# Rounding of quantised weights moved to ScalarE, activation tables loaded at named points, six tiles of a norm on ScalarE

## The reference, cut to what matters

```
x = x + tanh(g_xattn[l]) * xattn_l(layernorm(x), ctx_1024, ...)
x = x + tanh(g_ffn[l])   * ffn_l(layernorm(x), ...)
```

```
wq = clip(round(w / s_w), -128, 127) * s_w      # s_w = max|w| of the row / 127
xq = clip(round(x / s_x), lo, hi) * s_x         # s_x from the maximum of all of x
h  = silu(xq @ Wgate) * (xq @ Wup)              # layer 1 (352 hidden features)
h  = relu(xq @ W1 + b1)                         # layer 2 (512 hidden features)
y  = quantised(h) @ quantised(Wdown or W2)
```

## Time and profile before

| | |
|---|---|
| three runs | 1810.07, 1813.54, 1822.59 us, median 1813.54 us |
| the profiled execution | 1814.86 us, its span 1813.0 us |
| busy in the span | PE 72%, PEld 51%, DVE 64%, ACT 48%, POOL 24% |
| mean granted TensorE clock | 0.863 of full speed |
| table loads on ScalarE | 19 of 1283 ns |

### The profile page before, as it was taken

One profiled execution on the slowest core, in us unless ns is written; L12 is line 12 of the kernel. 1 busy time (PEld: TensorE's weight loads), 2 busy tenths in 40 slices (PEclk: granted clock), 3 DMA queues, 4 the chain that ended last, 5 costly groups with the idle time before them and its releaser, 6 DMA issues. The chain is left out here.

```text
span 1813.0 us, 32142 instructions
## 1 busy us (share of the span) xinstructions
PE 1304.0 (72%) x12243; PEld 922.2 (51%) x12245; DVE 1155.5 (64%) x2402; ACT 874.0 (48%) x1347; POOL 431.2 (24%) x635
## 2 busy tenths in 40 slices
PE   0898289999999992799999943389725788360774
PEld 0565156666666661577667731266514455230674
DVE  7565357777777775566666656576457577638444
ACT  3355237777777775455555533355334266210321
POOL 2243032222222210422222222134220100000552
PEclk9999589999999997699999985599956799755876
DMA  2342322222222322000000000222001221413434
GB/s 75 64 65 38 102 80 84 86 90 88 90 89 85 94 72 72 1 1 1 1 1 2 1 13 0 55 62 59 14 0 35 54 55 37 166 55 116 146 109 128
DMA packets 115349, 108.19 MB, mean 60 GB/s; under 512 B 44334, under 2 KB 98798, under 8 KB 114158
## 3 DMA queue, kind: packets, MB, share of 16 engines
q1 hardware_dynamic: 113150, 103.48, 20.4%
q0 software_dynamic: 2048, 2.65, 0.6%
HBM read 44.00 MB, written 8.71 MB: 29 GB/s over the span
## 5 line engine op out<-in xcount | busy, mean ns | idle before, releaser
L608 ACT ACTIVATE Pt<-bank 128x1024 f32<-128x1024 f32 (+1 forms) x384 | 366.5, 954 | 155.1 <-PE bank L552 151.0
L664 DVE TENSOR_REDUCE l0f_Mf<-bank 128x4 f32<-128x1024 f32 x192 | 234.4, 1221 | 101.7 <-PE bank L531 101.7
L572 PE MATMUL bank<-Pt,V 128*32 128x256 f32 (+1 forms) x3072 | 196.1, 374 | 11.1 <-POOL Pt L413 9.9
L1155 POOL TENSOR_TENSOR Psum<-Pt 128x512 f32<-128x512 f32 x64 | 83.4, 1303 | 236.2 <-ACT Pt L1289 236.2
L572 PEld LDWEIGHTS bank<-Pt,V 128*32 128x32 f32 x3072 | 81.2, 110 | 82.7 <-issue 26.2
L413 POOL TENSOR_SCALAR_AFFINE_SELECT Pt<-Pt 128x512 f32<-128x512 f32 x128 | 81.9, 640 | 171.3 <-ACT Pt L608 171.3
L1326 DVE TENSOR_TENSOR qk_lo<-bank,qk_hi 128x512 fp32r<-128x512 f32 x64 | 44.3, 692 | 107.3 <-ACT qk_hi L1281 107.3
L429 POOL CAST parts<-nodes 128x256 fp32r<-128x256 f32 x96 | 38.3, 399 | 300.6 <-PE bank L503 300.6
L552 PE MATMUL bank<-l0f_QK 64*128 64x256 f32 x768 | 97.6, 333 | 3.5 <-DMA l0f_QK<-l0f_NMrow 1.7
L664 DVE TENSOR_REDUCE l2x_Mf<-bank 128x4 f32<-128x1024 f32 x64 | 76.9, 1220 | 32.8 <-PE bank L531 32.7
L1289 ACT ACTIVATE Pt<-bank 128x1024 f32<-128x1024 f32 x64 | 65.6, 1025 | 57.3 <-PE bank L1230 57.3
(11 more groups left out here) (400 smaller groups left out, 3287.2 us busy)
## 6 DMA issues: line engine op xcount, KB each, us to landing
l0f_QK<-l0f_Z SPq DMA_DIRECT2D x288, 128.0 KB, 2.3
l2x_QK<-l2x_Z SPq DMA_DIRECT2D x96, 128.0 KB
V<-in_L_experts SPq DMA_DIRECT2D x8, 960.0 KB
Wg<-in_L_experts SPq DMA_DIRECT2D x8, 960.0 KB, 12.9
l0x_QK<-l0x_Z SPq DMA_DIRECT2D x48, 128.0 KB
tokB<-s_cand SPq DMA_DIRECT2D x16, 200.0 KB
s_y_even<-in_c_zero SPq DMA_DIRECT2D x1, 2048.0 KB, 11.1
s_y_odd<-in_c_zero SPq DMA_DIRECT2D x1, 2048.0 KB, 15.9
```

What stands on the lines that cost most here:

```text
L572: last = pe.matmul(bank[4][32 * x:32 * x + 32, o + q0:o + S], Va[:, 2 * n + k, 4 * j + x, :], Pp[:, (f + x // 2) % 4, x % 2, k * S:k * S + ...
L608: act.activation(Pp[:, g % 4, :, 0:w], banks[:, 2:4, 0:w], ACT.Exp, scale=L.scale).then_inc(exp_done, 1)
L664: d.tensor_reduce(m, A.rearrange("p h (t k) -> p h t k", t=2), AX, ALU.max).then_inc(max_done, 1)
L1155: e.tensor_tensor(Psum[:, q % 2], Pp[:, q % 4, :, 0:S], Pp[:, q % 4, :, S:2 * S], ALU.add).then_inc(key_sum, 1)
```

## The change

Eight edits:

1. `rstd_act` names the table set of the square root ahead of its wait for `ln_ask`.
2. `flow_act` names the set of the exponential at the loop's start.
3. A shared norm is split 10 to 6: VectorE normalises tiles 0 to 9, ScalarE 10 to 15.
4. Tanh of attention 1's gate goes from behind the norm (`l1x_act`) to the front of `l1x_in_act`, behind the wait for the loads, with a link.
5. In a quantised layer GpSimd's list loses the quantisation of the weights. ScalarE takes the first step (scale and add ROUND) of w1 and w2, as ACT.Copy with a scale by partition, and raises `h_scaled`; VectorE takes the other two, over all of w1 at once, between its fourth piece of x and the products of the scales.
6. The Exp for the clip factors of layer 1 goes behind the barrier and loses its link; VectorE waits for it ahead of its two instructions on `clip`.
7. ScalarE names Silu's set after the weights of layer 1.
8. In attentions 2 and 3 the last of the six slots is filled by GpSimd at the head of its list, and no longer by ScalarE.

```diff
         def rstd_act(a, n):
+            a.eng.preload_act_table_set("sqrt_and_others")
             a.eng.wait_ge(ln_ask, a.count("ln"))
...
-            half = NT // 2 if shared else NT
+            half = 10 if shared else NT
...
-            for t in range(NT // 2, NT):
+            for t in range(10, NT):
...
         def flow_act(a, L, base):
+            a.eng.preload_act_table_set("exp_and_others")
...
         def l1x_in_act(a):
             loaded(a, 8)
+            a.link(act.activation(g1[:], g1[:], ACT.Tanh))
...
         def l1x_act(a):
             ln_act(a, X, Qf)
-            a.link(act.activation(g1[:], g1[:], ACT.Tanh))
             a.barrier()
...
             everywhere_pool(0)
-            e.wait_ge(w_scaled, Q.i + 1)
-            W, Wq = w1[:, 0:Q.nw, 0:Q.nk, :], w1q[:, 0:Q.nw, 0:Q.nk, :]
-            for i in range(Q.nw):
-                for k in range(Q.nk):
-                    o = w1[:, i, k, :]
-                    g.link(e.tensor_scalar(o, o, iw1[:, i, k:k + 1], ROUND, ALU.mult, ALU.add))
-            for i in range(Q.nw):
-                g.link(e.tensor_scalar(W[:, i], W[:, i], ROUND, -128.0, ALU.subtract, ALU.max))
-                last = e.tensor_scalar(Wq[:, i], W[:, i], 127.0, None, ALU.min)
-                if i < Q.nw - 1:
-                    g.link(last)
-            last.then_inc(w_quant, 1)
-            o = w2[:, 0:Q.F]
-            g.link(e.tensor_scalar(o, o, sw2[:, 1:2], ROUND, ALU.mult, ALU.add))
-            g.link(e.tensor_scalar(o, o, ROUND, -128.0, ALU.subtract, ALU.max))
-            e.tensor_scalar(w2q[:, 0:Q.F], o, 127.0, None, ALU.min).then_inc(w_quant, 1)
             everywhere_pool(1)
...
             if Q.gated:
+                d.wait_ge(h_scaled, 1)
                 v.link(d.tensor_scalar(clip[:], clip[:], 1.0, None, ALU.add))
...
+            W, Wq, o = w1[:, 0:nw, 0:nk, :], w1q[:, 0:nw, 0:nk, :], w2[:, 0:F]
+            d.wait_ge(h_scaled, 7 * Q.i + Q.gated + 1)
+            v.link(d.tensor_scalar(W, W, ROUND, -128.0, ALU.subtract, ALU.max))
+            d.tensor_scalar(Wq, W, 127.0, None, ALU.min).then_inc(w_quant, 1)
+            d.wait_ge(h_scaled, 7 * Q.i + Q.gated + 2)
+            v.link(d.tensor_scalar(o, o, ROUND, -128.0, ALU.subtract, ALU.max))
+            d.tensor_scalar(w2q[:, 0:F], o, 127.0, None, ALU.min).then_inc(w_quant, 1)
             v.link(d.tensor_scalar(Sw, Sw, sx[:, 0:1], None, ALU.mult))
...
-                d.wait_ge(h_scaled, 4 * Q.i + c + 1)
+                d.wait_ge(h_scaled, 7 * Q.i + Q.gated + 3 + c)
...
             loaded(a, len(ffn_loads(Q)))
+            a.barrier()
             if Q.gated:
-                a.link(act.activation(clip[:], clip[:], ACT.Exp, scale=-1.0))
-            a.barrier()
+                act.activation(clip[:], clip[:], ACT.Exp, scale=-1.0).then_inc(h_scaled, 1)
+            act.wait_ge(w_scaled, Q.i + 1)
+            for i in range(Q.nw):
+                for k in range(Q.nk):
+                    o = w1[:, i, k, :]
+                    last = act.activation(o, o, ACT.Copy, bias=ROUND, scale=iw1[:, i, k:k + 1])
+            last.then_inc(h_scaled, 1)
+            o = w2[:, 0:Q.F]
+            act.activation(o, o, ACT.Copy, bias=ROUND, scale=sw2[:, 1:2]).then_inc(h_scaled, 1)
+            if Q.gated:
+                act.preload_act_table_set("silu_and_others")
             empty(a, "A", ffn_put_t(a, "A", Q), who=FFN_T)
...
             L = attentions[k]
+            g.eng.tensor_copy(L.QK[:, 2, :, 1, :], bc(rowk[:, 1:2].unsqueeze(1), [P, L.blocks, S]))
             values_ones(g, L)
...
                 a.eng.copy(v_view(L)[:, :, :, 0:L.dh], Kf[:].rearrange("p t (h d) -> p t h d", d=L.dh))
-                slots_blank(a, L, range(5, 6))
             if k == 3:
                 empty(a, "A", put_plain(a, "A", ocol))
-                slots_blank(a, L, range(5, 6))
```

## The result

Before: 1815.67 us, the median of four runs (1810.07 to 1822.59). After: 1787.32 us, the median of four (1779.72 to 1790.39). The ratio is 0.9844, 95% interval 0.9815 to 0.9873: 28.3 us less, between 23 and 34. The forecast was 1788.0. The profiled execution after took 1790.39 us, its span 1788.6 at a mean granted clock of 0.864.

What follows compares the result with a forecast made beforehand. No engine is busy all the time; barriers and chains of handovers bound the stages. Layer 1 12.7, layer 2 8.2, experts 1.7, attention 2 1.8, attention 1 1.6, nodes 0.8: 26.9 us off 1814.86 gives 1788, range 1780 to 1798.

Steps and rivals of the forecast that it cites:

- What bounds the weights' stage: Quantised layers, first maximum to first real matmul: a chain of handovers, no engine busy over 11.5 of 22.75 us.
- The shared norm: Ahead of quantised layers and experts: root's load off the path, 1.29 us, ten tiles to six, 0.44; together 1.73 each.
- Weights, layer 1 and layer 2: Rounding and clip moved off GpSimd bring w2's transposed copy earlier: 8.3 us (7.6 to 8.6) and 6.5 (6.0 to 6.8).
- Silu's set: Layer 1: the table load ahead of the first Silu moves under the quantisation, 1.28 us.
- Attention 1: Behind its norm load and Tanh go, 1.41 us, tiles 0.44; passage in costs 0.27; net 1.6 (0.3 to 1.6).
- Attention 2: Barrier ahead of the loop: without the sixth slot's copy ScalarE ends about 1.8 us earlier, still last; gain 1.3 to 1.8.
- The nodes' exponential: Nodes' loop: set named at its start saves 0.8 us, or 0 if the loop makes it up.
- Experts: Norm gains 1.7 us; a few experts more or fewer at the low clock move the time by up to 7 us.
- (a): Rival, table loads: they don't move, reloaded at the function or held by the same wait; 6 us less, 1794; 7%.
- (b): Rival, ScalarE: a set switch holds it longer than the load's row; 9 us more gain, 1779; 3%.
- (c): Rival, quantised layers: transposes or ScalarE, not GpSimd, delay the matmuls; about half of 8.3 and 6.5 stays, 1795; 4%.
- (d): Rival, experts: TensorE's granted clock makes the change slower from 15 of 32 more experts at the low level; 2%.

Runs made afterwards that it cites:

- the kernel with the small instructions: Before, without GpSimd's first reduction across partitions (a copy instead), plus two small tensor_scalar instructions heading each layer's GpSimd list: 1810.44 us, one run.

## Why the prediction was right

- **What bounds the weights' stage.** Right: handovers, and GpSimd last. With the weights alone moved, 8.9 and 7.2 us went. What the 6.92 us of idle time ahead of GpSimd's first weight instruction were, I had left open.
- **The shared norm.** Forecast 1.73 us a norm (1.29 for the load, 0.44 for the tiles). Measured 1.86 in layer 2 and 1.88 in the experts, and 3.25 in layer 1 with Exp, forecast 3.14. VectorE ends last, as worked out. There are 21 loads instead of 19. One of the two is a named set that stood already: the root's ahead of attention 3, which now starts 4.94 us after the norm's start instead of 4.60, so 0.34 us where I took nothing (the prediction had named a load that appears twice as a sign of being wrong; this one is small). The other stands ahead of the root of attention 1 and costs nothing: the prediction says that the set stands there, but Tanh, moved ahead of it, had switched it.
- **Weights, layer 1 and layer 2.** Forecast 8.3 (7.6 to 8.6) and 6.5 (6.0 to 6.8), measured 8.95 and 7.17: above both bounds. The terms were mis-sized in three places. In layer 1 VectorE's four instructions took 1.61 us from the end of x to what followed, not 2.0: 0.55 us on 768 elements, where the line of the earlier trace rows gave 0.635. That line ended on a row of 1536 elements at 1.22 us, and 2048 elements take the same 1.22 in the profile of before; a line to that row would have given 0.57. The copy of w2 ended 0.27 us behind VectorE's copy of x, not 0.45 (they overlap); 0.1 of this was lost again ahead of the copy of x. And x was quantised 0.15 us sooner, without GpSimd beside it. In layer 2 the four took 1.60 us, not 1.87, the small products behind them 1.16 without GpSimd instead of 1.40 beside it, and the copy of w2 0.33 instead of 0.5.
- **Silu's set.** Forecast 1.28; behind the copies layer 1 is 1.34 us shorter, and no load stands ahead of the first Silu.
- **Attention 1.** Head 11.3 to 9.42 us: 1.9, forecast 1.85. Tanh at 711.92 takes 0.20 us on the way in, its load stands in the idle time ahead, as taken; the passage's 17.3 to 17.9 us against 17.1 to 17.7 cannot resolve the 0.27.
- **Attention 2.** The barrier of its loop comes after 15.1 to 15.6 us, before after 17.2 to 17.3: 1.6 to 2.1, forecast 1.8. The whole stage does not show it: 165.3 to 167.6 and 165.2 to 168.4. Over all kernels with this edit, nine profiles, it took 163.3 to 168.4, mean 165.3, against a mean of 166.6 in the five without. Its loop's spread is larger than the gain, or gives part of it back; that stays open.
- **The nodes' exponential.** Forecast 0.8, not found: the band of the nodes is the same, and taking the edit out moved neither it nor the whole time. It was allowed for ("or 0 if the loop makes it up"). That the edit would touch attention 0 the prediction does not say.
- **Experts.** The norm as forecast; the 2.45 us at the head not. The prediction put the clock's width on the loop over the experts ("four experts either way", 7 us). On these chips the loop varies by 20 us in one and the same kernel, three times as much, and the granted clock in the rows does go with it; only the comparison on one chip takes it out.
- **Bounds of the sum.** The bounds given with the terms add up to 23.0 and 27.5 us, not to 21 and 28, which leaves the range, 1780 to 1798, about as it is.
- **Rivals.** (a) fell: the root follows its request by 0.1 us. (b) predicted 9 us more gain; the joints leave no room for it, 3.25 against 3.14 where two switches left the path. The drain of about 1.38 us that the Trainium skill, ScalarE: Activation LUTs, section "What ACT_TABLE_LOAD costs", puts beside each load did not show up as a gain when the load was moved. (c) fell with the weights alone. (d) did not occur; the experts were faster.

The joints together: 13.5 + 9.1 + 1.9 (attention 1) + 1.9 (experts' norm), which repeat within 0.1 us, are 26.4 us; with the 2.45 us of the head 28.9, and up to 2 more if attention 2 keeps its part. The measured 28.3 us, with 5 either way, hold that. The mechanism of the prediction was right, and its sum was 26.9; that the median fell within 1 us of 1788 is in part luck. For the two layers and the experts' norm 22.6 us were forecast and 24.5 came, the 2.45 us of the experts' head were not forecast, the nodes' 0.8 did not come, and attention 2's 1.8 is not resolved in its stage.

## What to carry to other kernels

Cut profiles at landmarks and compare stages across several profiles before explaining any: what repeats within 0.1 us belongs to the code, what moves by 3 to 20 us in an unchanged kernel need not. Where the lengths fall into groups, as those of attention 0 do, compare the groups and not the ranges. Where an engine idles for "issue" ahead of an instruction, ask what ran on it before that kind of instruction last ran, and either take the delay early with a tiny instruction of the kind or move the work away. Once a chain of handovers is gone, read the order of each list again: here VectorE's part of the weights was worth another 2.4 us, TensorE's fixed order of transposes 1.1 and a clip that cannot act 5.9.

## What the runs showed of the hardware that was not expected

- GpSimd's first tensor_scalar behind a reduction across partitions is held for 6.9 to 7.9 us, even 200 us and many copies later; memset, copy, affine select and (in after, at the head of attention 2) cast are not held.
- The delay had an accidental use. VectorE's instructions on 512 elements take 0.43 to 0.49 us alone. With GpSimd's weights beside them, once its delay was gone, they took up to 0.76 in layer 1 and 0.80 in layer 2. Two of the latter, from the kernel with the small instructions:

```profile
1332.35 0.71 DVE L1511 TENSOR_SCALAR O<-O 128x512 f32<-128x512 f32 x1
1333.09 0.80 DVE L1512 TENSOR_SCALAR xq<-O 128x512 bf16<-128x512 f32 x1
```

- The same 80 matmuls of the experts' head took 18.5, 21.5 or 23.9 us of TensorE's busy time, by how many of them ran at the lower level, and the length of that stretch repeated to 0.02 us in two executions of before and three of after. A norm 1.9 us shorter or a delay of 4 us ahead of the burst thus went with 2.5 or 3.0 us less behind it.
- Attention 0, whose matmuls are the same in all kernels, has three lengths, about 199, 202 and 205 us, at a granted clock of 0.94, 0.91 and 0.88 to 0.90 from 50 us on; with Exp's set named at the head of its loop none of eight executions had the middle one.
